# Table loads split by partition, and one-hot ids spread through TensorE

## The reference

```
e = stack([tbl_f[ids[:, f]] for f in 0..25], axis=1)        # 512 x 26 x 128
combined = concatenate([dense[:, None, :], e], axis=1)      # 512 x 27 x 128
inter = einsum('bfd,bgd->bfg', combined, combined)          # upper triangle: 351 numbers
h = concatenate([dense, inter_flat, dense], axis=1)         # 512 x 607
h = relu(h @ W_top1 + b_top1); h = relu(h @ W_top2 + b_top2); y = h @ W_top3
```

## Time and profile before

| | |
|---|---|
| median of three runs | 181.42 us (180.19 to 184.68) |
| the profiled execution, its span | 181.4 us |
| TensorE products, busy | 115.4 us (64%) |
| GpSimd, busy | 79.6 us (44%) |
| ScalarE, busy | 71.9 us (40%) |
| VectorE, busy | 71.7 us (40%) |
| mean granted TensorE clock | 0.802 |
| moved by DMA | 12.67 MB, mean 70 GB/s |

### The profile page before, as it was taken

The page is one execution under the profiler, slowest core; times in us unless marked ns, Lnnn a source line. Parts: engine busy times, 40 slices in busy tenths (PEclk is TensorE's granted clock), DMA queues, the critical chain, the costliest instruction groups (busy, mean ns, idle before and its releaser), DMA issues.

```text
span 181.4 us, 1866 instructions
## 1 busy us (share of the span) xinstructions
PE 115.4 (64%) x694; PEld 98.3 (54%) x694; DVE 71.7 (40%) x119; ACT 71.9 (40%) x112; POOL 79.6 (44%) x84
## 2 busy tenths in 40 slices
PE   6177746952814000099889571398785959797795
PEld 6164525832603000078789461197685957797692
DVE  4173476632320011186294400265624643164430
ACT  0465098545042000378664400235541462265422
POOL 1777777777777776073787777000000000000000
PEclk9858975996575555558999955558999999999999
DMA  4956456859831121010112121000000000000000
GB/s 90 260 173 192 150 170 172 186 188 241 251 120 44 44 58 43 14 47 18 54 29 59 46 58 52 20 0 0 4 0 0 0 0 4 0 0 4 0 0 0
DMA packets 5738, 12.67 MB, mean 70 GB/s; under 512 B 1849, under 2 KB 2361, under 8 KB 5602
## 3 DMA queue, kind: packets, MB, share of 16 engines
q1 hardware_dynamic: 3010, 7.26, 13.6%
q0 software_dynamic: 2432, 4.99, 10.3%
q10 hardware_dynamic: 288, 0.32, 0.9%
HBM read 12.55 MB, written 0.00 MB: 69 GB/s over the span
## 4 chain that ended last, share of the span: by engine, by line
PE 46%; another core or an unknown queue 22%; issue 9%; DVE 9%; DMA 7%; ACT 6%; SPq 1%; ACTq 0%; DVEq 0%
PE gram L416 14%; PE late L386 8%; DMA table<-in_tbl 7%; PE late L387 7%; PE gram L432 3%; DVE dots L564 3%; PE look L396 3%; PE late L450 2%; DVE onehot L729 2%; PE late L452 2%; PE late L451 2%; PE look L488 1%; DVE w_lo L803 1%; ACT table_hi L587 1%
## 5 line engine op out<-in xcount | busy, mean ns | idle before, releaser
L341 POOL DMA_INDIRECT e_rows<-in_tbl,idx x76 | 78.8, 1036 | 33.4 <-issue 22.6
L386 PE MATMUL late<-onehot,table_hi 125*128 125x512 f32 x56 | 29.1, 519 | 41.3 <-DVE onehot L729 21.6
L416 PE MATMUL gram<-eT 128*123 128x104 f32 x256 | 35.1, 298 | 11.3 <-issue 8.4
L416 PEld LDWEIGHTS gram<-eT 128*123 128x123 f32 x256 | 33.2, 213 | 12.8 <-issue 9.4
L386 PEld LDWEIGHTS late<-onehot,table_hi 125*128 125x128 f32 x56 | 14.0, 250 | 47.5 <-ACT eT L587 26.1
L729 DVE TENSOR_SCALAR onehot<-ids,row_of_partition 125x512 fp32r<-125x512 int32 x42 | 19.3, 497 | 36.7 <-remote 23.6
L587 ACT ACTIVATE dots<-gram 32x208 f32<-32x208 f32 x32 | 16.5, 517 | 35.3 <-PE gram L416 20.0
L564 DVE COPY dots<-gram 32x208 f32<-32x208 f32 (+1 forms) x32 | 16.5, 516 | 28.7 <-remote 14.9
L387 PE MATMUL late<-onehot,table_lo 125*128 125x512 f32 x56 | 27.2, 486 | 0.0
L607 ACT ACTIVATE onehot<-distance 125x512 fp32r<-125x512 f32 x14 | 8.8, 631 | 27.2 <-remote 24.3
L556 DVE COPY eT<-look 128x512 f32<-128x512 f32 (+1 forms) x12 | 11.7, 972 | 10.8 <-PE look L396 7.5
(11 more groups left out here) (49 smaller groups left out, 109.1 us busy)
## 6 DMA issues: line engine op xcount, KB each, us to landing
table<-in_tbl SPq DMA_DIRECT2D x6, 500.0 KB
ids<-in_ids_bcast SPq DMA_DIRECT2D x6, 256.0 KB
w_raw<-in_w SPq DMA_DIRECT2D x1, 1280.0 KB
e_rows<-in_tbl,idx POOLq DMA_INDIRECT x76
w_raw<-in_w SPq DMA_DIRECT2D x1, 512.0 KB
table<-in_tbl SPq DMA_DIRECT2D x2, 250.0 KB
ids<-in_ids_bcast ACTq DMA_DIRECT2D x1, 256.0 KB
x_rows<-in_dense SPq DMA_DIRECT2D x1, 256.0 KB
```

Of the source, the lines that this page charges most:

```text
L341: pool.indirect_dma_start(out=e_rows[:, t % 2, s, :], out_offset=None, in_=tables[f][:, :], in_offset=bass.IndirectOffsetOnAxis(ap=idx[:, ...
L386: pe.matmul(bank, table_hi[0:KP, i % 2, c, :], hot, start=c == 0, stop=False)
L416: last = pe.matmul(gram[0:ROWS_OUT, n % 2, q, 0:QUADS * NG_COL], eT_flat[:, b * SLOTS:b * SLOTS + ROWS_OUT], eT[:, b:b + QUADS, 0:NG_COL], ...
```

## The change

Four edits, in two groups.

**Table loads.** Each load of a table, and each of the two pieces of table 0, becomes two DMAs: partitions 0 to 111 and partitions 112 to 124. The waits on their semaphores count both.

**Ids.** The seven broadcast loads go. One DMA of 7 partitions (14 KB), issued by ScalarE behind the index load, brings the ids of the seven tables. GpSimd builds `pick_f` (7 x 7 x 128: block i is one in row i, zero elsewhere) ahead of its gathers. VectorE rounds `pick` and the ids, two instructions ahead of its first one-hot. TensorE then makes 14 products of 7 rows (`spread_ids(i)`: `pick` of table i times the ids, 128x512), one into a bank of `gram` for ScalarE and one for VectorE: tables 0 and 1 before the first one-hot product, table i+2 after the product of table i. ScalarE and VectorE compare from these PSUM banks (two per engine, in turn), and wait for `ids_full`, which TensorE raises, in place of the DMA semaphores.

```
+            pool.memset(pick_f[:, :, :], 1.0).then_inc(pick_ready, 1)
+            pool.wait_ge(pick_ready, 1)
+            pool.affine_select(out=pick_f[:, :, :], in_=pick_f[:, :, :], compare_op=ALU.is_equal, fill=0.0,
+                               base=0, pattern=[[-1, NOH], [0, P]], channel_multiplier=1).then_inc(pick_ready, 1)
...
-                sp.dma_start(table[0:KP, i % 2, 0:c, :],
-                             tables[ONE_HOT[i]].rearrange("(p c) d -> p c d", c=c)).then_inc(table_in[i % 2], 16)
-            def load_ids(i):
...
+                rows = tables[ONE_HOT[i]].rearrange("(p c) d -> p c d", c=c)
+                for lo, hi in ((0, SPLIT_P), (SPLIT_P, KP)):
+                    sp.dma_start(table[lo:hi, i % 2, 0:c, :], rows[lo:hi, :, :]).then_inc(table_in[i % 2], 16)
...
+        def ids_bank(i, eng):
+            return gram[:, eng, i % IDS_RING * 4:i % IDS_RING * 4 + 4, :].rearrange("p q c -> p (q c)")
...
+            def spread_ids(i):
+                for eng in (FOR_ACT, FOR_DVE):
+                    last = pe.matmul(ids_bank(i, eng), pick[:, i, :], ids_f[:, :], start=True, stop=True)
+                last.then_inc(ids_full, 1)
...
+            pe.wait_ge(pick_rounded, 2)
+            for i in range(IDS_AHEAD):
+                spread_ids(i)
             for i in range(NOH):
                 one_hot_product(i)
+                if i + IDS_AHEAD < NOH:
+                    spread_ids(i + IDS_AHEAD)
...
-                act.activation(distance[0:KP, n % 2, :], ids[0:KP, i % IDS_RING, :], ACT.Abs,
+                act.activation(distance[0:KP, n % 2, :], ids_bank(i, FOR_ACT)[0:KP, :], ACT.Abs,
...
-            act.dma_start(ids[:, 0, :], ids_bcast[ONE_HOT[0]:ONE_HOT[0] + 1, :].to_broadcast([P, B])
-                          ).then_inc(ids_in[0], 16)
+            act.dma_start(ids_in_sb[:, :], ids_hot).then_inc(ids_in, 16)
...
-                dve.tensor_scalar(onehot[0:KP, n % OH_RING, :], ids[0:KP, i % IDS_RING, :],
+                dve.tensor_scalar(onehot[0:KP, n % OH_RING, :], ids_bank(i, FOR_DVE)[0:KP, :],
...
+            dve.wait_ge(pick_ready, 2)
+            dve.tensor_copy(pick[:, :, :], pick_f[:, :, :]).then_inc(pick_rounded, 1)
+            dve.wait_ge(ids_in, 16)
+            dve.tensor_copy(ids_f[:, :], ids_in_sb[:, :]).then_inc(pick_rounded, 1)
...
-                    dve.wait_ge(ids_in[(i + 1) % IDS_RING], 16 * ((i + 1) // IDS_RING + 1))
+                    dve.wait_ge(ids_full, i + 2)
```

More of the change, by code:

```diff
@@ L63 @@
 K1 = KT + 1
-OH_RING, IDS_RING = 8, 4
+OH_RING, IDS_RING = 8, 2
+FOR_ACT, FOR_DVE = 0, 1
+SPLIT_P = 112
+IDS_AHEAD = 2
 WARM_UP = 9
@@ L159, with build @@
 ROWS_OUT = 3 * 32 + NF
-def build(nc, dense, ids_rows, ids_bcast, tables, w1, w2, b2, w3, out):
+def build(nc, dense, ids_rows, ids_hot, tables, w1, w2, b2, w3, out):
     with ExitStack() as ctx:
@@ L170, in build @@
         idx = sb("idx", [P, TILES, NTAB], I32)
-        ids = sb("ids", [P, IDS_RING, B], I32)
+        ids_in_sb = sb("ids_in_sb", [NOH, B], I32)
+        ids_f = sb("ids_f", [NOH, B], F32R)
+        pick_f = sb("pick_f", [NOH, NOH, P])
+        pick = sb("pick", [NOH, NOH, P], F32R)
         row0 = {c: sb(f"row_of_partition_{c}", [P, c]) for c in sorted(set(CHUNKS))}
@@ L207, in build @@
         idx_in = sem("idx_in")
-        ids_in = [sem(f"ids_in{k}") for k in range(IDS_RING)]
+        ids_in = sem("ids_in")
+        pick_ready = sem("pick_ready")
+        pick_rounded = sem("pick_rounded")
+        ids_full = sem("ids_full")
         table0_in = [sem(f"table0_in{k}") for k in range(2)]
@@ L291, in load_table @@
                     sp.wait_ge(lo_ready, pieces_split(i - 2))
-                sp.dma_start(table[0:KP, i % 2, 0:c, :],
-                             tables[ONE_HOT[i]].rearrange("(p c) d -> p c d", c=c)).then_inc(table_in[i % 2], 16)
-            def load_ids(i):
-                if i >= IDS_RING:
-                    sp.wait_ge(onehot_dve, chunks_made(DVE_CHUNK, i - IDS_RING))
-                    sp.wait_ge(onehot_act, chunks_made(ACT_CHUNK, i - IDS_RING))
-                sp.dma_start(ids[:, i % IDS_RING, :], ids_bcast[ONE_HOT[i]:ONE_HOT[i] + 1, :].to_broadcast([P, B])
-                             ).then_inc(ids_in[i % IDS_RING], 16)
+                rows = tables[ONE_HOT[i]].rearrange("(p c) d -> p c d", c=c)
+                for lo, hi in ((0, SPLIT_P), (SPLIT_P, KP)):
+                    sp.dma_start(table[lo:hi, i % 2, 0:c, :], rows[lo:hi, :, :]).then_inc(table_in[i % 2], 16)
             for k, (a, c) in enumerate(PIECES[0]):
-                sp.dma_start(table[0:KP, 0, a:c, :], tables[ONE_HOT[0]].rearrange(
-                    "(p c) d -> p c d", c=CHUNKS[0])[:, a:c, :]).then_inc(table0_in[k], 16)
-            load_ids(1)
+                rows = tables[ONE_HOT[0]].rearrange("(p c) d -> p c d", c=CHUNKS[0])
+                for lo, hi in ((0, SPLIT_P), (SPLIT_P, KP)):
+                    sp.dma_start(table[lo:hi, 0, a:c, :], rows[lo:hi, a:c, :]).then_inc(table0_in[k], 16)
             load_table(1)
             sp.dma_start(x_rows[:, :, :], dense.rearrange("(t p) d -> p t d", p=P)).then_inc(x_in, 16)
-            load_ids(2)
-            load_ids(3)
             for i in range(2, NOH):
                 load_table(i)
-                if i + 2 < NOH:
-                    load_ids(i + 2)
                 if i == NOH - 1:
@@ L593, in split_hi @@
                     if i == 0:
-                        act.wait_ge(table0_in[k], 16)
+                        act.wait_ge(table0_in[k], 16 * 2)
                     else:
-                        act.wait_ge(table_in[i % 2], 16 * (i // 2 + i % 2))
+                        act.wait_ge(table_in[i % 2], 16 * 2 * (i // 2 + i % 2))
                     copy(table_hi[0:KP, i % 2, a:c, :], table[0:KP, i % 2, a:c, :]).then_inc(hi_ready, 1)
@@ L627, in one_hots @@
                     if c == ACT_CHUNK[0][1]:
-                        act.wait_ge(ids_in[i % IDS_RING], 16 * (i // IDS_RING + 1))
+                        act.wait_ge(ids_full, i + 1)
                     one_hot(i, c)
@@ L744, in _ @@
             mine = [c for a, c in DVE_CHUNK if a == 0]
-            dve.wait_ge(ids_in[0], 16)
+            dve.wait_ge(ids_full, 1)
             one_hots(0, mine[:2])
@@ L847 @@
         "ids_rows": np.ascontiguousarray(ids.reshape(TILES, P, NTAB).transpose(1, 0, 2)),
-        "ids_bcast": np.ascontiguousarray(ids.T),
+        "ids_hot": np.ascontiguousarray(ids.T[ONE_HOT]),
         "w1": np.ascontiguousarray(w1_rows.reshape(K1 + 1, P, H1).transpose(1, 0, 2)),
@@ L860 @@
     out = nc.dram_tensor("out_y", (1, B), F32, kind="ExternalOutput").ap()
-    build(nc, ap["dense"], ap["ids_rows"], ap["ids_bcast"], [ap[f"tbl_{f}"] for f in range(NTAB)],
+    build(nc, ap["dense"], ap["ids_rows"], ap["ids_hot"], [ap[f"tbl_{f}"] for f in range(NTAB)],
           ap["w1"], ap["w2"], ap["b2"], ap["w3"], out)
```

## The result

The change gave no gain. The kernel after takes 184.15 us (median of 4 runs, 182.37 to 184.97), the kernel before took 180.85 us beside it (4 runs, 180.19 to 184.68); the ratio is 1.017, interval 1.009 to 1.026. A second set of runs of the same two kernels, 181.95 against 181.43 us, gave 1.003 (0.994 to 1.011). The forecast was 176 and faster. The profiled execution of after has a span of 183.2 us.

What follows compares the result with a forecast made beforehand. Loads bound the front, then two holes following GpSimd, then a fixed 64.4 us tail. Pauses 3 us shorter and gathers 2.5 shorter put the last gather at 108.3, copies at 111.5, end 176 us; own range 171 to 181, overall 148 to 189.

Steps and rivals of the forecast that it cites:

- The front's lead and its fate: Table stretch: 4.3 us ahead when lateness begins; 3 us off GpSimd's pauses, last gather at about 108.3, end 175.9.
- the lateness: One-hot and gram stretches: TensorE's reports of finished work reach other engines some 20 us late, 3.5 us a chunk; inferred.
- The bound of 6.7: Front, tables 0 to 3: most that faster loads can gain, 28.3 us against 21.6 at 5.4 us a table.
- Split loads: Table loads: 1.6 us instead of 3.8 to 5.1, hidden behind the engines' pace; removes 9.4 us of ScalarE's waits.
- Ids at the start: Before the first one-hot: VectorE's 5.0 us wait for ids goes, a shorter chain replaces it; gain 1.3 us.
- Compare from PSUM: VectorE's one-hots: 0.62 us each instead of 0.497, 5.2 us over 42, 0.75 us a table counted in full.
- Shorter gathers: GpSimd's 76 gathers: part of their 7 us excess lies beside VectorE's one-hots; 2.5 us gained, bounds 0 and 5.
- The fixed tail: From 117 us to the end: TensorE's own 64.4 us, no gather left, untouched by the change.
- Case 3: Whole kernel: front's gain eaten by added pairs, or split halves share engines, and GpSimd's pauses stay; 181 us, chance 0.22.
- the added pairs: TensorE's fourteen ids products: 1.5 us cost in the front; in the late stretch 3.5 us more lateness a pair.
- Case 2: Both holes: lateness is a matter of traffic and goes wholly or partly; 132 us for both, 144 or 165; chance 0.22.
- the 45 us of holes: TensorE's idle stretches, 54 to 76.5 and 98 to 117 us; forecast to follow GpSimd and stay; their start unexplained.

Runs made afterwards that it cites:

- late executions: Runs on three chips where the kernel before took 181.4 to 183.4 us with waits for "remote"; on one chip, without such waits, it took 138.9 and 138.8.
- tied: Kernel after, with gathers of group n (3 to 9) waiting until group n-3 is turned: 182.54 us, ratio 0.998; where nothing is late 135.66 us, 0.977.
- compares from SBUF: Kernel after, with VectorE copying each table's ids from PSUM into SBUF and comparing there: 185.88 us, no ratio, beside 181.43 before.

## Why the prediction was wrong

Two of its steps failed: the size of the front's lead, and above all what becomes of it.

**The front's lead and its fate. This is the step that failed.** The sum put the lead at 4.3 us after table 3, let it reach the lateness, and passed it on through shorter pauses of GpSimd to a last gather at 108.3. The lead was more than that: 9.2 us after table 2, of which 1.2 are an earlier first product (10.19 to 8.98) and 8.0 the pace (three tables in 15.9 us instead of 23.9). Where nothing is late it is 10.1 us after table 3 (39.0 to 28.9). The bound of 6.7 rested on 5.4 us a table, and the kernel after takes 5.3 and less with the dearer compares and the added products in it; the 3.75 us taken off for these don't show. But the lateness, which the text took to begin near table 3 as before, began with table 2, by 21 to 27 us. Table 3 ended 8 us later than before. GpSimd's pauses, from which I took 3 us, grew by 2.4. The last gather ended at 112.8, and the end came at 183.2 instead of 175.9.

A faster front doesn't carry a gain into a stretch whose onset isn't fixed: in five late executions with gathers as close as here, the first wait of more than 2 us for "remote" ended anywhere from 20 us (after, second set) over 22 (tied), 27 (after) and 40 (before) to 85 (compares from SBUF), and the span was 181 to 185 us in all. Whether the 14 products have a part in the loss isn't shown. Where nothing is late the only wait for them is VectorE's first one, 1.7 us; in the late stretch ScalarE waits 3.25 us for a pair, up to 48.48. Neither half of the change was run alone in late executions.

**Split loads: the sign came, the cause is only half.** The DMA view of the kernel after, by fortieth of 9 to 14 us, as the earlier trace rows:

```profile
DMA  9610000000099614093448989998795977765410
GB/s 328 164 33 0 0 0 0 0 0 0 0 229 131 66 66 98 33 229 131 164 197 361 426 361 459 262 229 229 197 262 131 262 230 197 197 197 164 131 33 0
```

The load of table 2, issued from 9.51 on, reaches 9 tenths and up to 459 GB/s and is over by 14 us, where before 2 or 3 tenths went on. The forecast gave this to the split; the split alone left 10.0 us from issue to use, and the removed broadcasts had the larger part. The rule against splitting by partitions that the forecast cited (the Trainium skill, page "DMA: Bandwidth & Descriptors") gives as its reason that both halves spray across all 16 engines. The whole loads of 125 partitions here keep only 2 or 3 tenths of the engines busy, and splitting alone gained 1.2%.

**Ids at the start: the number near, the cause wrong.** Gain forecast 1.3, measured 1.7 (first one-hot 8.61 to 6.87). But with the ids alone the first one-hot stands at 8.60, where it was. The gain is the split loads'. The two extra GpSimd instructions were indeed hidden: its first gather started at 4.42, before at 4.94.

**Compare from PSUM: mis-sized.** 0.62 us taken, 0.745 measured, 10.4 us in all instead of 5.2. I took a value between the two rows; the upper one (0.69 for a VectorE read of PSUM) was itself too low. That it counts in full, 0.75 us a table, was wrong as well: with compares from SBUF table 6 is through at 44.6, with compares from PSUM at 45.8 where nothing is late, 1.2 us for all tables (on two chips). The estimate by the Trainium skill, page "VectorE: DVE Perf Modes", section on mode 2x_2P, was an increase of 0.26 us a compare; the trace shows 0.248 (0.745 less 0.497), so for the difference the page was nearer than my interpolation, though both levels that the forecast worked out from its clock alone (0.53 and 0.27) lie some 0.22 us under the rows.

**Shorter gathers: the size right.** 2.5 us forecast, 2.5 measured (78.8 to 76.3); without lateness 2.9 (80.3 to 77.4). The forecast gave it to VectorE's compares alone. The split of the loads, alone, brings as much (1.7 us) as the ids part alone (1.8).

**The fixed tail: wrong by 2.9 us.** I took 64.4 us as a constant. The work was the same, the granted clock was not (0.94, then 0.90). Three more late executions with the changed kernel's products in the tail have one as long: 67.3 us in the second set (clock 0.90), 67.1 with compares from SBUF (0.90), 68.5 tied (0.88). So it may belong to the change; for the kernel before there is one late trace, and I can't tell.

**The rivals.** Case 3 (nothing gets to the end, 181 us, 0.22) is what happened, by its outcome. Of the causes that it named, the split halves gained time, and the added pairs are open. Case 2 (the lateness is a matter of traffic, 132 us for both holes) was a good number by luck: 133.8 us is the span where nothing is late, but there the kernel before has no holes either. So the 45 us of holes were never a property of this kernel's schedule alone. I read them out of one chip's executions, and "the holes follow GpSimd" made me leave them be, when it was the lever: a slower GpSimd takes them away. The chances for faster add up to 0.52 and for same to 0.30, where the text has 0.51 and 0.31.

What stays open is what in the hardware makes TensorE's reports fall behind, and why one chip of the four doesn't show it. Shown is that it needs the gathers, depends on their pace, and ends with them. Fills and pauses slow GpSimd's issuing and the gathers' traffic together, so which of the two matters isn't shown. That it is TensorE's reports which are late rests on order: its products are done, and those who wait for them start in a bunch afterwards. No row names the queue.

## What to carry to other kernels

Where waits are put down to "remote" and end shortly after another engine falls silent, don't plan around them: slow that engine a little, by a small fill or by waiting for its own landings, and see whether the whole kernel gets faster, on more than one chip, since where nothing is late the slower engine is a loss by my estimate. Cut no corner ahead of such a stretch until it is gone, since it swallows what is gained before it. And one chip's profile doesn't show which holes are the kernel's own: here the same change was worth +1.7%, +0.3% and -2.3% of time in three sets of runs.

## What the runs showed of the hardware

- 76 gathers of 128 rows, 1.25 us apart where nothing stretches them, go with waits for "remote" of up to 46 us on three chips of four; 1.25 and 1.44 in turn do so too, and 1.44 throughout hardly (4.7 us at most). 0.2 us more for each gather took the changed kernel from some 182 to 184 us down to 152.6.
- The hole moves with small edits (it is 46 us long in the tied kernel), while the end hardly moves.
- A load of 500 KB over 125 partitions, beside gathers, took 11.8 us from issue to use beside broadcasts of ids, 10.0 split by partitions, 7.2 without the broadcasts, and at most 5.0 with both edits.
- A VectorE compare of 125x512 takes 0.745 us from PSUM and 0.487 to 0.497 from SBUF; in one pair of kernels those from SBUF cost the gathers 0.059 us each, 4.5 us over 76, and in two other pairs, where broadcasts went as well, 1.2 and 1.8 us.
- A pause until the last gather has landed lasts 1.8 to 3.3 us where only gathers move, and up to 5.4 us beside table loads.
